# A transformer block with gated linear attention: rewritten opening, with all modulation rows in it

## The reference

```python
x = L0_attn_hidden_states                                  # 4 x 256 x 512
mod = (_silu(L0_c) @ L0_wmod).reshape(4, 6, 1, -1)
sa, ca, ga, sb, cb, gb = (mod[:, i] for i in range(6))
ga = (2 * (ga >= 0) - 1) * jnp.maximum(jnp.abs(ga), 0.25)  # gb the same
h = _layernorm(x, axis=-1) * (1 + ca) + sa
x = x + ga * attention(h)
h = _layernorm(x, axis=-1) * (1 + cb) + sb
x = x + gb * ffn(h)
```

## Time and profile before

| | |
|---|---|
| median of 3 runs | 1099.9 us (1098.33 to 1103.17) |
| the profiled execution | 1100.45 us, its span 1098.7 us |
| mean granted clock of TensorE | 0.979 |
| busy: PE, DVE, ACT, POOL | 1045.7, 816.6, 696.6, 224.2 us |

### The profile page before, as it was taken

The page is one execution under the profiler, slowest core; times in us unless marked ns, Lnnn a source line. Parts: engine busy times, 40 slices in busy tenths (PEclk is TensorE's granted clock), DMA queues, the critical chain, the costliest instruction groups (busy, mean ns, idle before and its releaser), DMA issues. The chain is left out here.

```text
span 1098.7 us, 14605 instructions
## 1 busy us (share of the span) xinstructions
PE 1045.7 (95%) x4680; PEld 808.4 (74%) x4680; DVE 816.6 (74%) x1585; ACT 696.6 (63%) x1368; POOL 224.2 (20%) x140
## 2 busy tenths in 40 slices
PE   5879999999999999999999999999997859999898
PEld 1657777777777777877777777787774349888786
DVE  5777887888888788878888887887878785444412
ACT  3448877887787788778878787877874434222300
POOL 3412212222211131122222112211323410000000
PEclk9989999999999999999999999999998969999999
DMA  6122301310131122013101311220123231111011
GB/s 226 55 67 80 112 20 38 100 53 19 38 115 39 33 85 91 19 38 115 38 19 38 126 44 40 77 76 19 45 72 135 76 129 45 57 38 58 29 39 38
DMA packets 37464, 70.89 MB, mean 65 GB/s; under 512 B 2936, under 2 KB 19576, under 8 KB 35520
## 3 DMA queue, kind: packets, MB, share of 16 engines
q1 hardware_dynamic: 36720, 70.16, 19.8%
q10 hardware_dynamic: 720, 0.43, 0.1%
HBM read 68.33 MB, written 2.24 MB: 64 GB/s over the span
## 5 line engine op out<-in xcount | busy, mean ns | idle before, releaser
L1373 POOL TENSOR_TENSOR q_sin<-q_sin,cst 128x512 f32<-128x512 f32 x64 | 88.9, 1388 | 311.7 <-ACT q_sin L764 311.7
L1213 DVE SCALAR_TENSOR_TENSOR prob<-ps_s,scal,dec 128x128 f32<-128x128 f32 x256 | 71.9, 343 | 77.6 <-PE ps_s L670 77.6
L1361 POOL TENSOR_TENSOR dec<-dec,future 128x1024 f32<-128x1024 f32 x31 | 74.5, 2402 | 265.9 <-ACT expg L783 265.9
L54 PE MATMUL ps_q<-hT_hi,wq_hi 128*128 128x512 f32 x256 | 125.5, 490 | 3.3 <-DVE q_cos L1023 2.5
L54 PE MATMUL ps_o<-wo_hi,z_hi 128*128 128x512 f32 x260 | 103.8, 399 | 2.5 <-DVE z_lo L49 2.4
L54 PE MATMUL ps_gt<-hT_hi,wg_hi 128*128 128x512 f32 x256 | 103.8, 405 | 2.0 <-DVE sg L1043 2.0
L56 PE MATMUL ps_o<-wo_hi,z_lo 128*128 128x512 f32 x260 | 103.4, 398 | 0.0
L55 PE MATMUL ps_o<-wo_lo,z_hi 128*128 128x512 f32 x260 | 103.2, 397 | 0.0
L56 PE MATMUL ps_q<-hT_hi,wq_lo 128*128 128x512 f32 x256 | 101.2, 395 | 0.0
L55 PE MATMUL ps_gt<-hT_lo,wg_hi 128*128 128x512 f32 x256 | 101.1, 395 | 0.0
L56 PE MATMUL ps_gt<-hT_hi,wg_lo 128*128 128x512 f32 x256 | 100.7, 393 | 0.0
(11 more groups left out here) (251 smaller groups left out, 2737.6 us busy)
## 6 DMA issues: line engine op xcount, KB each, us to landing
dec<-gT_dram SPq DMA_DIRECT2D x32, 512.0 KB, 5.5
raw_q<-wq_in SPq DMA_DIRECT2D x32, 256.0 KB, 2.7
raw_g<-wg_in SPq DMA_DIRECT2D x32, 256.0 KB, 2.9
raw_o<-wo_in SPq DMA_DIRECT2D x8, 1024.0 KB, 6.9
raw_pair<-wkv_in SPq DMA_DIRECT2D x8, 512.0 KB, 4.7
raw_pair<-wgu_in SPq DMA_DIRECT2D x6, 512.0 KB, 3.2
raw_gu<-wgu_in SPq DMA_DIRECT2D x5, 512.0 KB, 3.4
qT<-wmod_in SPq DMA_DIRECT2D x2, 1024.0 KB, 6.9
```

Of the source, the lines that this page charges most:

```text
L54: pe.matmul(out, w_hi, x_hi, start=first, stop=False)
L1213: last = nc.vector.scalar_tensor_tensor(prob[:, h], ps_s[:, h * P:(h + 1) * P], scal[:, tile, 1, h:h + 1], dec[:, tile // 2 % 2, h, tile % ...
L1361: nc.gpsimd.tensor_tensor(cells, cells, future[:].unsqueeze(1).broadcast_to([P, GRP * CPB, CHUNK]), ALU.add).then_inc(mask_done, 1)
L1373: nc.gpsimd.tensor_tensor(q2, q2, sinT, ALU.mult).then_inc(qsin_done, 1)
```

## The change

All six modulation rows are made in the opening. A row's four products are no longer summed by TensorE: each writes 32 partitions of its own (`silu_c` has 32 columns for each, of which 4 are not zero), and the turn, with a matrix that picks four rows of each 32, sums them (`sel`). SA and CA come first, SB behind q block -3, CB behind g block -3, GA behind q block -2, GB behind g block -2. Layer norm works by batches of two tiles: ACT modulates 128x256 at a time, GpSimd subtracts for batches 0 and 1 with 128x1024 elements, VectorE for 2 and 3. The softplus argument stands ahead of the first q block, in `ps_o` and `ps_s`. All four heads of the first group are loaded without a wait into `raw_first` (which takes the place of `wo_hi` and `wo_lo`), their high parts are made by ACT, their low parts by VectorE. The gates are bounded with the channels on the partitions (128x32) and stored in DRAM by elements. x is loaded again for the residual, and the gate for all partitions, before the tail begins; GpSimd multiplies and adds tile by tile.

```diff
-        silu_c = sb("silu_c", [P, KT * B])
+        silu_c = sb("silu_c", [P, KT, LANE])
...
+        wmod = {SA: qT[:, 0], CA: sg[:, 0], SB: qT[:, 1], CB: sg[:, 1], GA: x1[:, 0:4], GB: x1[:, 4:8]}
+        ps_rows = {SA: ps_q[:], CA: ps_g[:], SB: ps_y, CB: ps_y, GA: ps_y, GB: ps_y}
+        mod_part = [part[:].rearrange("p h i -> p (h i)") for part in (z, expg)]
+        ps_zT = [ps_o[:], ps_s]
...
@@ sync
             sp.dma_start(cT, cT_in).then_inc(c_loaded, 16)
-            for half, m in enumerate((SA, CA)):
-                load_mod(m)
-                a = half * NT // 2
-                sp.dma_start(x1[:, a:a + NT // 2], x_in[a:a + NT // 2].rearrange("t p n -> p t n"))\
-                    .then_inc(x_loaded[half], 16)
+            load_x(0)
+            load_mod(SA)
+            load_mod(CA)
+            load_x(1)
             load_kv(0)
-            load_head(0, 0, True)
+            load_first(0)
             sp.dma_start(cst[:, C_COST:C_TRI], cst_in[:, C_COST:C_TRI]).then_inc(tables_loaded, 16)
-            for j in range(1, GRP):
-                load_head(0, j)
+            load_first(1)
+            load_mod(SB)
+            load_mod(CB)
+            load_first(2)
+            load_first(3)
+            sp.wait_ge(ln_turned, B)
+            load_mod(GA)
+            load_mod(GB)
...
+            sp.wait_ge(guard, GUARD_END)
+            for i in range(2):
+                sp.dma_start(modrow[i].rearrange("(m p) -> p m", p=P),
+                             gate_T[:, i].rearrange("p b k -> p (b k)"),
+                             allow_slow_non_contiguous=True).then_inc(rows_stored, 16)
@@ tensor
-            def mod_row(m):
-
-                pe.wait_ge(mod_loaded[m], 16 * KT if m == GB else 16)
+            def mod_rows(m):
+
+                pe.wait_ge(mod_loaded[m], 16)
                 for k in range(KT):
-                    last = nc.tensor.matmul(ps_rows[m], silu_c[:, k * B:(k + 1) * B], weights(m, k),
-                                            start=k == 0, stop=k == KT - 1)
-                last.then_inc(rows_ready, 1)
+                    nc.tensor.matmul(ps_rows[m][k * LANE:(k + 1) * LANE], silu_c[:, k], wmod[m][:, k],
+                                     start=True, stop=True).then_inc(rows_ready, 1)
...
+            def mod_turn(slot, count):
+
+                pe.wait_ge(rows_copied, count)
+                part = mod_part[(count - 1) % 2]
+                for k in range(KT):
+                    last = nc.tensor.matmul(ps_modT[:, slot, k], part[:, k * P:(k + 1) * P], sel,
+                                            start=True, stop=True)
+                last.then_inc(mod_turned, 1)
...
+            kv_chunk(0, -1, 0)
+            ln_turn(2)
+            kv_chunk(0, -1, 1)
+            ln_turn(3)
...
+            softplus_argument(0)
+            pe.wait_ge(ln_lo[1], 2)
+            softplus_argument(1)
             q_block(0, -4, True)
+            k_turn(0, -1)
             g_block(0, -4, 0, KT, True)
...
+            softplus_turn()
             q_block(0, -3)
-            softplus_turn()
+            mod_rows(SB)
+            pe.wait_ge(zT_copied, 1)
+            mod_turn(2, 3)
             g_block(0, -3, 0, KT)
...
+            mod_rows(CB)
+            pe.wait_ge(late_modT_done, 1)
+            mod_turn(3, 4)
             pe.wait_ge(ones_done, 1)
             cumulative()
+            q_block(0, -2)
...
+            mod_rows(GA)
...
+            mod_turn(4, 5)
+            g_block(0, -2, 0, KT)
...
+            mod_rows(GB)
+            mod_turn(5, 6)
             q_block(0, -1)
             g_block(0, -1, 0, KT)
@@ tensor, tail
-                    mod_row(GA)
...
-                    mod_row(CB)
-                if t == 7:
-                    mod_row(GB)
...
-                if t == 5:
-                    mod_row(SB)
-                if t == 7:
-                    mod_turn(ps_late_modT, late_rows, 4)
@@ vector
+            first_lo(1)
+            rotate_q_cos(0, -4)
+            softplus_before_exp()
+            rotate_q_add(0, -4)
+            cap(0, -4)
+            softplus_argument_of_series()
+            softplus_series(0)
+            softplus_series(1)
+            gate(0, -4)
+            decay_rates()
+            first_lo(2)
+            rotate_q_cos(0, -3)
@@ vector, tail
-                    guard_gate(0)
...
-                    guard_gate(1)
@@ gpsimd
-            for t in range(NT):
-                norm.pool_split_lo(pool, t)
+            for b in range(2):
+                ln_lo_half(b)
```

556 lines of the change are left out of this document (296 added, 260 removed).

## The result

| | before | after |
|---|---|---|
| median of 4 runs | 1099.1 us (1096.9 to 1103.2) | 1124.05 us (1121.2 to 1127.4) |
| the profiled execution | 1100.45, span 1098.7 | 1124.04, span 1122.1 |

A forecast was written before the change was run, and what follows sets the result against it. TensorE was taken to be busy throughout the 749.0 us loop, with slack only in opening and tail. Sum: 1099.9 + 8.0 (opening) + 0 (tail) = 1107.9, given as 1108, slower by 0.7%; range 1093 to 1117.

The forecast's parts named there:

- nothing can be won or lost: Loop over the heads: 749.0 us with TensorE busy throughout and its body unchanged, so no gain or loss.
- Up to the first modulation: Start of the opening: first modulation at 20.6 against 19.73 before, late by 0.9 us.
- the 4.3 that the sum has for SA: Opening: row SA's products take 4.3 us, from 11.0 to 15.3.
- a product's own two passes can't: Opening rows: a product's own two passes can't overlap, leaving five steps of eight, 2.2 us for four products.
- rival (a): Opening rows: column groups run fully side by side, 0.9 instead of 2.2 us a row; 1094.0 in all, chance 0.2.
- Up to 48.2: Opening to the end of first q block, g block and softplus argument: 48.2 against 46.4, late by 1.8 in all.
- Up to the first scores: Rest of the opening: 31.7 us of work and 6.7 of waits, ending at 86.6; opening longer by 8.0.
- rival (d): Half clock in opening and tail: up to 2 and 4 us more, 1114 in all; chance 0.1.
- The tail: End of the attention: 3.7 us gained without the rows, 3.7 lost to the clock (bounds 0 and 7.5), net 0.
- The gates' store: Two transfers of 2048 4-byte elements, issued before the loop on its feeding queue: 0 us, bounds 0 and 4.
- A loop longer than 749 (then the store of the gates is to blame): Sign that the forecast is wrong: loop above 749 us, blamed on storing the gates.
- the feed-forward part isn't touched: Feed-forward part behind 896.6 us: the change leaves it alone, so no gain or loss.

The follow-up runs named there:

- a_fill: The changed kernel with products whose result nobody reads in four of TensorE's waits in the opening, between 50 and 86 us: 1117.7 us.
- b_pad: The kernel before with 32 bytes of padding ahead of its first SBUF table and nothing else: 1109.9 us.
- a_tailfill: The changed kernel with products whose result nobody reads in TensorE's waits in the attention's tail: 1117.8 us.
- a_pad: The changed kernel with 32 bytes of padding ahead of its first SBUF table: 1120.5 us.
- a_pad4064: The changed kernel with 4064 bytes of padding ahead of its first SBUF table: 1112.1 us.
- a_early: The changed kernel with the second part of the opening in another order, all six rows computed, SB and CB before 37 us: 1122.1 us.

## Why the prediction was right or wrong

The direction was right (0.55 for slower), the size was not: 1124 lies 7 us above the range. Two terms that the sum put at nothing failed: the clock in the opening (7.5 us in the profile), and the loop and the feed-forward part, where "nothing can be won or lost" (10.7). Step by step:

- **Up to the first modulation**, late by 0.9: it is 0.5 early (19.21). No run shows the 4.3 that the sum has for SA: its products took 1.94 and ended at 12.3, at a granted clock of 1.00 in the profile, as in the 6.30 of the kernel before. CA's ended at 15.3 and not 17.7. The step "a product's own two passes can't" run beside the next product's failed: they do, as rival (a) had it. Four products side by side had 3.60 / 1.06 = 3.4 times the speed here.
- **Up to 48.2**, late by 1.8: it is 46.3. The long subtractions met as forecast (GpSimd 2.72 for 128x1024, VectorE 3.25 for what took 2.17 in the earlier trace rows, the two rows below); the gain came from the earlier start and the batches (the last normalised tile at 32, not 34).

```profile
21.95 2.72 POOL L51 TENSOR_TENSOR hT_lo<-dec,hT_hi 128x1024 fp32r<-128x1024 f32 x1 [19.44 <-DVE hT_hi L46]
```
```profile
22.50 3.25 DVE L51 TENSOR_TENSOR wkv_lo<-raw_pair,wkv_hi 128x1024 fp32r<-128x1024 f32 x1
```

- **Up to the first scores**, 31.7 of work and 6.7 of waits from 48.2 to 86.6: it is 46.3 to 93.0. Start -1.9, rows -3.2 (1.06 + 1.0 each instead of 2.2 + 0.65), waits +4.0 (10.7), and the clock +7.5: TensorE is busy for 35.97, where the work at full clock is 28.5. These four make up the 6.4. The failed term is the clock, left at 0 in the sum and put at 2 in rival (d); a_fill gave 6.7 for it. The mechanism was named, and its price was in the row of the kernel before with passes of 0.63, which the sum took for a thing of that kernel. 7.5 us of clock on 10.7 of waits: each us waited had to be counted as 1.7, and as 1.4 to 2.0 over the six profiles with the same waits, so how large the miss came out was partly luck.
- **Rival (a)** had its mechanism right and its time wrong: full overlap would end the opening at 76.4 if ACT's copies came at once. They did not: SB's stands in ACT's order behind a head's split and two swaps (it starts at 52.52, the row ended at 50.70), the others behind swaps or the sigmoid.
- **The tail**, 3.7 gained and 3.7 lost to the clock, 0: the two profiles give -1.7, but ten profiles with the changed tail have 66.9 to 69.4 and the old one has 69.5 and 66.9 (b_pad), so 0 stands. No run shows the 2.5 for each of three out products, nor the half of 7.5 that was taken: the kernel before has one slow one, the last (5.5 us from 887.00 on, its passes at 0.63 or more), and the stretch that was slow half-way is row CB's in the kernel before, at a mean granted clock of 0.61 from 850.7 to 856.5. a_tailfill gives what half clock costs the changed tail as 5.8 (67.9 to 62.1), within the bounds of 0 and 7.5. How much of that the old tail lost too, and so how large the gain of 3.7 really was, no run tells apart.
- **The gates' store**, 0 with bounds 0 and 4: 1.7 in the changed kernel, nothing in a_pad and a_pad4064, 5.25 in a_early. "A loop longer than 749 (then the store of the gates is to blame)" named the sign and a wrong cause for three quarters of it.
- **"Nothing can be won or lost there"**, of the loop, and "the feed-forward part isn't touched": the largest unnamed miss, 8.9 us. Both have the same instructions on operands that were moved, and b_pad shows that this is enough (9.1 us with 32 bytes).

In sum against the profiled execution: 8.0 forecast for opening and tail, 12.7 measured; 0 for the rest, 10.7 measured. In the opening 1.9 and 3.2 us of gains that the prediction didn't have hide part of what it missed in waits and clock (11.5).

## What to carry to other kernels

Where TensorE is busy throughout, a change elsewhere can still cost (here a pair of steps took 25.13 us instead of 24.95): compare the pitch of the same products before and after, not only idle time, and if it moved, try padding ahead of the operands (here 4064 bytes gave 24.93) before judging the change. Several waits of some 2 us on TensorE cost more than their sum here (1.4 to 2.0 times), for some of the blocks behind them ran at the lower clock (0.53 to 0.59); unread products in the waits gave that back (6.7 and 5.8 us), and they belong into both kernels of a comparison. Small work moved out of a stage with waits into a stage with an ordered queue pays for the copy behind it, not for itself: put its consumer a block later than its producer. And before GpSimd is given a long memset (here 3.51 us), look at what VectorE does beside it (an operation of 0.29 took 4.83).
